# Splitting the row maxima of an attention step as columns on GpSimd before they are turned, and storing them with two transfers

## The reference, cut to what matters

```python
q, k, v = x @ Wq.T, x @ Wk.T, x @ Wv.T           # x: (4, 512, 256) after the layer norm
scores = einsum('bsqhd,bthd->bqhst', qh, kh) * scale     # qh: (4, 512, 4, 8, 8), kh: (4, 512, 8, 8)
probs  = softmax(scores, axis=-1)
a_dot  = einsum('bqhst,bthd->bsqhd', probs, vh)
out    = a_dot * (1 - w) + a_mem * w              # a_mem from elu(q) @ memory
# + moe_forward(x): top 2 of 8 experts (256 -> 1024 -> 512 -> 256) + a shared expert (256 -> 1024 -> 256)
```

## Time and profile before

| | us |
|---|---|
| median of three runs | 819.31 |
| the runs | 809.73 to 820.09 |
| the profiled execution | 819.6 |
| its span, first to last instruction | 817.8 |
| mean granted TensorE clock in it | 0.985 |

### The profile page before, as it was taken

One profiled execution on the slowest core, in us unless ns is written; L12 is line 12 of the kernel. 1 busy time (PEld: TensorE's weight loads), 2 busy tenths in 40 slices (PEclk: granted clock), 3 DMA queues, 4 the chain that ended last, 5 costly groups with the idle time before them and its releaser, 6 DMA issues.

```text
span 817.8 us, 14331 instructions
## 1 busy us (share of the span) xinstructions
PE 711.9 (87%) x3976; PEld 371.2 (45%) x3977; DVE 586.4 (72%) x800; ACT 482.2 (59%) x886; POOL 150.6 (18%) x265
## 2 busy tenths in 40 slices
PE   4999999667788888888888888889999999998997
PEld 2455445211122221122122211368777778777887
DVE  4375688657688888888988884376677676675764
ACT  2473401456678878778877778655556555555422
POOL 1000001746452122211222212000000000003750
PEclk9999999879799999999999999999999999999999
DMA  9637000435320011111011163041111111113431
GB/s 318 212 103 282 30 0 16 139 126 191 100 82 28 19 30 30 30 30 30 16 29 30 43 219 108 13 137 51 50 39 51 51 38 51 46 38 111 123 104 51
DMA packets 51295, 65.36 MB, mean 80 GB/s; under 512 B 9512, under 2 KB 44224, under 8 KB 51264
## 3 DMA queue, kind: packets, MB, share of 16 engines
q1 hardware_dynamic: 40192, 40.85, 15.7%
q10 hardware_dynamic: 8000, 15.73, 5.9%
q0 software_dynamic: 3072, 8.39, 3.3%
HBM read 40.15 MB, written 24.38 MB: 79 GB/s over the span
## 4 chain that ended last, share of the span: by engine, by line
PE 58%; issue 13%; ACT 10%; DVE 7%; POOL 4%; DMA 3%; SPq 3%; DVEq 2%; ACTq 1%; POOLq 0%
PE ps L1374 10%; PE ps L1345 9%; PE ps L1226 7%; ACT att L718 6%; PE ps L1398 6%; PE ps L1476 5%; PE ps L1444 5%; DVE smax L980 4%; PE ps L1218 3%; PE ps L1491 3%; ACT att_r L698 2%; DMA att<-m_parts 2%; SPq L407 2%; PE ps L1251 2%; PE ps L1186 2%
## 5 line engine op out<-in xcount | busy, mean ns | idle before, releaser
L980 DVE TENSOR_REDUCE smax<-ps 128x2 f32<-128x1024 f32 x256 | 302.4, 1221 | 64.5 <-PE ps L1251 62.3
L718 ACT ACTIVATE att<-ps 128x512 f32<-128x512 f32 x512 | 267.7, 602 | 102.0 <-PE ps L1398 100.8
L1398 PE MATMUL ps<-att 51*128 51x512 bf16 x512 | 163.0, 390 | 63.9 <-ACT att L718 23.4
L1251 PE MATMUL ps<-att 48*128 48x512 bf16 x512 | 160.7, 391 | 1.4 <-DVE smax L980 1.4
L1398 PEld LDWEIGHTS ps<-att 51*128 51x128 bf16 x512 | 40.1, 94 | 254.4 <-DVE smax L980 104.0
L1345 PE MATMUL ps<-att,v_head 128*32 128x512 f32 x1024 | 139.2, 616 | 1.6 <-ACT o_sb L677 0.6
L1037 DVE TENSOR_TENSOR att_r<-big,att_r 128x1024 fp32r<-128x1024 f32 x76 | 89.8, 1222 | 60.4 <-ACT att_r L698 60.4
L1374 PE MATMUL ps<-att_r 128*128 128x512 f32 x456 | 115.8, 403 | 15.3 <-DVE att_r L1041 13.6
L1374 PEld LDWEIGHTS ps<-att_r 128*128 128x128 f32 x456 | 84.1, 188 | 39.5 <-issue 19.6
L698 ACT ACTIVATE att_r<-big 128x1024 fp32r x74 | 74.4, 1053 | 19.6 <-issue 17.6
L584 POOL DMA_INDIRECT xn<-slot_y,slot x32 | 33.8, 1056 | 229.1 <-DMA slot_y<-xn 219.6
(11 more groups left out here) (162 smaller groups left out, 711.2 us busy)
## 6 DMA issues: line engine op xcount, KB each, us to landing
big<-w ACTq DMA_DIRECT2D x8, 1024.0 KB, 5.6
q_stacks<-big SPq DMA_DIRECT2D x12, 512.0 KB
att<-q_stacks SPq DMA_DIRECT2D x64, 96.0 KB, 2.1
slot_x<-zeros SPq DMA_DIRECT2D x1, 4992.0 KB, 17.2
e_x<-slot_x SPq DMA_DIRECT2D x39, 128.0 KB, 2.0
slot_y<-xn SPq DMA_DIRECT2D x39, 128.0 KB, 1.7
big<-w ACTq DMA_DIRECT2D x8, 512.0 KB, 8.1
att<-k_stacks SPq DMA_DIRECT2D x64, 48.0 KB, 2.0
```

What stands on the lines that cost most here:

```text
L718: act.activation(probs[:, t % 2, g, :], ps[:, RING[turn_of(u) % 3], :], ACT.Exp, scale=SCALE)\
L980: dve.reduce_max(smax[:, s % 2, :].rearrange("p (half v) -> p half v", half=2)[:, :, v], ps[:, bank:bank + 2, :], X_AXIS).then_inc(max_don ...
L1251: return pe.matmul(ps[:, bank + half, :], q_st[s][rows, g, P * st:P * (st + 1)], k_st[s][rows, :], start=True, stop=True)
L1398: pe.matmul(ps[:, RING[turn % 3], :], k_st[s][rows, P * t:P * (t + 1)], q_st[s][rows, g, :], start=True, stop=True).then_inc(scores_ready, 1)
```

## The change

- transpose_max is now an ordinary bf16 matmul: its stationary operand is max_parts (128 x 48), the moving one `eye`, a bf16 copy of the identity that GpSimd makes at the start. It gives 48 x 128: per half, three parts of eight rows.
- The split stands before it: split_max on GpSimd takes smax as it is (128 partitions x 16) once all eight maxima are there, in the same four operations, each waiting for the one before, and writes the parts into max_parts. It waits for the matmul that read the buffer two steps before.
- negate_max on ScalarE negates 48 x 128 and rounds to bf16 (neg_parts), which is exact. It waits for the transfers that read that buffer.
- m_rows waits for the negation and issues two transfers of three rows instead of six of one.
- On TensorE, in step(), transpose_max comes behind weighted_values of that quarter instead of ahead of it; it waits for the last split operation.
- On GpSimd split_max(i) comes ahead of stage_v(i) and of the scatters instead of between them.
- VectorE's first maximum of a step waits for the split that read the buffer, no longer for the matmul.

```diff
@@ -127,9 +127,11 @@
         expert = sb("expert", [P, TILES], I32)
         mden = sb("mden", [P, 2, 2, G])
         smax = sb("smax", [P, 2, 16])
-        negm = sb("negm", [16, 2, P])
-        negr = sb("negr", [16, 2, P])
-        m_parts = sb("m_parts", [16, 2, 3, P], BF16)
+
+        max_parts = sb("max_parts", [P, 2, 48], BF16)
+        max_rest = sb("max_rest", [P, 16])
+        neg_parts = sb("neg_parts", [48, 2, P], BF16)
+        eye = sb("eye", [P, P], BF16)
         rden = sb("rden", [P, 2, 32])
         oT_sb = sb("oT_sb", [P, 2, 32, DH + 1])
         otmp = sb("otmp", [P, 2, 32, DH])
@@ -207,6 +209,7 @@
         router_zero = sem("router_zero")
         ident_zero = sem("ident_zero")
         ident_ready = sem("ident_ready")
+        eye_ready = sem("eye_ready")
         consts_ready = sem("consts_ready")
         slots_cleared = sem("slots_cleared")
         dve_step = sem("dve_step")
@@ -400,12 +403,11 @@
                       .then_inc(stack_loaded[n], 16)
 
             def m_rows(i, s):
-                sp.wait_ge(m_ready, i + 1)
+                sp.wait_ge(negm_ready, i + 1)
                 for half in range(2):
-                    for c in range(3):
-                        row = HALF * half + R + c
-                        sp.dma_start(q_st[s % 4][row:row + 1, :, :].rearrange("o g s -> o (g s)"),
-                                     m_parts[8 * half:8 * half + 8, s % 2, c, :]).then_inc(m_loaded[s % 2], 16)
+                    first = HALF * half + R
+                    sp.dma_start(q_st[s % 4][first:first + 3, :, :].rearrange("c g n -> c (g n)"),
+                                 neg_parts[24 * half:24 * half + 24, s % 2, :]).then_inc(m_loaded[s % 2], 16)
 
             sp.wait_ge(s_hused, NF)
             load_stack(0, 0, 0)
@@ -480,6 +482,8 @@
             pool.wait_ge(ident_zero, 1)
             pool.affine_select(out=ident[:, :], in_=ident[:, :], compare_op=ALU.not_equal, fill=1.0,
                                base=0, pattern=[[-1, P]], channel_multiplier=1).then_inc(ident_ready, 1)
+            pool.wait_ge(ident_ready, 1)
+            pool.tensor_copy(eye[:, :], ident[:, :]).then_inc(eye_ready, 1)
             pool.memset(router[:, :, :], 0.0).then_inc(router_zero, 1)
             pool.memset(mem_w[:, :], 0.0).then_inc(mem_zero, 1)
             pool.memset(zeros[:, :], 0.0)
@@ -512,19 +516,22 @@
                 pool.tensor_copy(v_head[:, s % 2, :, first:first + DH],
                                  v_all[:, bass.ds(b * ST, ST), bass.ds(h * DH, DH)]).then_inc(v_head_ready, 1)
 
-            def split_m(i, s, pairs):
+            def split_max(i, s):
 
                 a = s % 2
-                pool.wait_ge(negm_ready, i + 1)
-                wait(pool, m_loaded[a], pairs * 96)
-                pool.tensor_tensor(m_parts[:, a, 0, :], negm[:, a, :], zeros[0:16, 0:P], ALU.subtract).then_inc(m_hi, 1)
+                whole, rest = [m.rearrange("p (half v) -> p half v", half=2) for m in (smax[:, a, :], max_rest[:, :])]
+                hi, mid, lo = [max_parts[:, a, :].rearrange("p (half c v) -> p half c v", half=2, c=3)[:, :, c, :]
+                               for c in range(3)]
+                nothing = zeros[:, 0:16].rearrange("p (half v) -> p half v", half=2)
+                pool.wait_ge(max_done, i * 8 + 8)
+                wait(pool, maxT_in_psum, i - 1)
+                pool.tensor_tensor(hi, whole, nothing, ALU.subtract).then_inc(m_hi, 1)
                 pool.wait_ge(m_hi, i + 1)
-                pool.tensor_tensor(negr[:, a, :], negm[:, a, :], m_parts[:, a, 0, :], ALU.subtract).then_inc(m_res, 1)
+                pool.tensor_tensor(rest, whole, hi, ALU.subtract).then_inc(m_res, 1)
                 pool.wait_ge(m_res, i + 1)
-                pool.tensor_tensor(m_parts[:, a, 1, :], negr[:, a, :], zeros[0:16, 0:P], ALU.subtract).then_inc(m_mid, 1)
+                pool.tensor_tensor(mid, rest, nothing, ALU.subtract).then_inc(m_mid, 1)
                 pool.wait_ge(m_mid, i + 1)
-                pool.tensor_tensor(m_parts[:, a, 2, :], negr[:, a, :], m_parts[:, a, 1, :], ALU.subtract)\
-                    .then_inc(m_ready, 1)
+                pool.tensor_tensor(lo, rest, mid, ALU.subtract).then_inc(m_ready, 1)
 
             def add_o(pair, a, b, h):
 
@@ -535,8 +542,8 @@
                                    otmp[:, a, :, :].rearrange("p (t g two) d -> p t g (two d)", t=ST, g=G),
                                    ALU.add).then_inc(o_added, 1)
 
+            split_max(0, 0)
             stage_v(0, 0, 0, 0)
-            split_m(0, 0, 0)
 
 
             pool.wait_ge(s_add, 2 * 4)
@@ -557,8 +564,8 @@
                 for s in range(4):
                     i = blk * 4 + s
                     if not (first and s == 0):
+                        split_max(i, s)
                         stage_v(i, b, h0 + s, s)
-                        split_m(i, s, blk * 2 + s // 2)
                     if isinstance(i, int) and 1 <= i < 8:
                         scatter(*SCATTERS[i])
                     if s == 1 and not first:
@@ -665,10 +672,10 @@
                         between[n, f]()
 
 
-            def negate_max(i, s):
+            def negate_max(i, s, pairs):
                 act.wait_ge(maxT_in_psum, i + 1)
-                wait(act, m_ready, i - 1)
-                act.activation(negm[:, s % 2, :], ps[0:16, RING[MAX_AT % 3], 0:P], ACT.Copy, scale=-1.0)\
+                wait(act, m_loaded[s % 2], pairs * 32)
+                act.activation(neg_parts[:, s % 2, :], ps[0:48, RING[MAX_AT % 3], 0:P], ACT.Copy, scale=-1.0)\
                    .then_inc(negm_ready, 1)
 
             def evacuate_o(pair, a):
@@ -703,7 +710,7 @@
                 for u in range(16):
                     t, g = divmod(u, G)
                     if u == 4 and not last:
-                        negate_max(i + 1, s + 1)
+                        negate_max(i + 1, s + 1, blk * 2 + (s + 1) // 2)
                     if u == 7 and last:
                         act.wait_ge(scattered, 16 * TOPK * NT)
                         copy_ex(0, 0)
@@ -724,7 +731,7 @@
                 act.dma_start(w2_sb[:, n, :, :], w2[n].rearrange("(k p) n -> p k n", p=P)).then_inc(w12_loaded, 16)
 
             LATE = {-4: (4, 5), -3: (6,), -2: (7,), -1: ()}
-            negate_max(0, 0)
+            negate_max(0, 0, 0)
             for i in range(4):
                 exps(0, i, first=i == 0)
                 if i == 0:
@@ -976,7 +983,7 @@
 
                 dve.wait_ge(a_ready, i * 8 + (v + 1))
                 if v == 0:
-                    wait(dve, maxT_in_psum, i - 1)
+                    wait(dve, m_ready, i - 1)
                 dve.reduce_max(smax[:, s % 2, :].rearrange("p (half v) -> p half v", half=2)[:, :, v],
                                ps[:, bank:bank + 2, :], X_AXIS).then_inc(max_done, 1)
 
@@ -1159,6 +1166,7 @@
         @block.tensor
         def _(pe):
             pe.wait_ge(ident_ready, 1)
+            pe.wait_ge(eye_ready, 1)
 
             def transpose_xn(g):
 
@@ -1298,9 +1306,9 @@
                     wait(pe, probs_ready, i * 16 + (v + 1))
 
             def transpose_max(i, s):
-                pe.wait_ge(max_done, i * 8 + 8)
+                pe.wait_ge(m_ready, i + 1)
                 bank_free(i - 1, MAX_AT)
-                pe.transpose(ps[0:16, RING[MAX_AT % 3], 0:P], smax[:, s % 2, :], ident[:, :])\
+                pe.matmul(ps[0:48, RING[MAX_AT % 3], 0:P], max_parts[:, s % 2, :], eye[:, :], start=True, stop=True)\
                   .then_inc(maxT_in_psum, 1)
 
             shared_down(1, NF - 1)
@@ -1378,7 +1386,7 @@
             def step(blk, s, first=False, ahead=True, last=False):
                 i = blk * 4 + s
                 pair = blk * 2 + s // 2
-                pe.wait_ge(m_loaded[s % 2], blk * 192 + 96 * (s // 2 + 1))
+                pe.wait_ge(m_loaded[s % 2], blk * 64 + 32 * (s // 2 + 1))
                 for t in range(ST):
                     for g in range(PAIR):
                         v = PAIR * t + g
@@ -1401,8 +1409,6 @@
                                 ins = max_scores((s + 2) % 4, v, 1 - half, 2 * (v % 2))
                                 if half == 1:
                                     ins.then_inc(a_ready, 1)
-                    if t == MAX_AT // G - 1 and not last:
-                        transpose_max(i + 1, s + 1)
                     if t == OUT_AT // G - 1 and s % 2 == 0 and not first:
                         transpose_o(pair - 1, (s // 2 + 1) % 2)
 
@@ -1410,6 +1416,8 @@
                         weighted_values(i, s, t - 1, pair)
                     elif not first:
                         weighted_values(i - 1, s + 3, ST - 1)
+                    if t == MAX_AT // G - 1 and not last:
+                        transpose_max(i + 1, s + 1)
 
                     if last and t == 0:
                         pe.wait_ge(experts_known, 1)
```

## The result

| | before | after |
|---|---|---|
| median, us | 817.8 (4 runs, 809.73 to 820.09) | 792.14 (4 runs, 791.57 to 793.09) |
| ratio | | 0.9705, 95% interval 0.9635 to 0.9774 |
| the profiled execution, us | 819.6 | 791.59 |
| its span, us | 817.8 | 789.8 |
| mean granted clock | 0.985 | 0.995 |

The kernel is 3.0% faster. 792.14 is 5 us above the forecast of 787 and inside its range. The median of before lies between 809.24 and 817.8 in the sets of runs of this document; those of after, in its two sets, are 0.07 us apart. Of the 28.0 us between the two spans, 17.7 are gained by the start of step 6 (230.69 against 212.97), 9.3 in steps 6 to 27, and 1.0 in the last four steps; behind the attention both kernels take the same time.

What follows compares the result with a forecast made beforehand. No engine is full; steps are chains of hand-overs in a three-bank PSUM ring, with waits for rows. Gains of 20.3 us by step 6, 11.5 in steps 6 to 27 and 0.9 at the end give 787 us; range 778 to 800.

Steps and rivals of the forecast that it cites:

- hidden 0.57 us: Ahead of even loop steps: TensorE waits 0.57 us a pair for row transfers, not the eighth maximum; all of it goes.
- The signs named in the forecast: No row waits ahead of steps 1, 2, 4; full clock 150 to 220 us; 21.2 us pairs; timely split; 2 us gap.
- the risk in its last sentence: Step 0: if the TensorE gap near 148 lowers the clock as long waits did, 1.2 us are lost.
- B: GpSimd's split is late for the turning matmul: 802 us at 0.45 us an operation, 790 at 0.33; chance 0.2.
- D: Same split, each operation far dearer: all gain lost at 0.60 us, 836 us total at 0.74; chance 0.03.
- C: Early steps: rows or stack still land late beside expert load, scatter and stack loads; 797 us, chance 0.12.
- E: Little gain: even steps really wait for the maximum, early waits come from loads beside the rows; 814 us, chance 0.05.
- a quarter of the 0.23 us between two of 512 columns: Turning matmul on TensorE: a bf16 matmul of 128 columns should hold it for 0.06 us.
- The upper bound, 0.21: Turning matmul on TensorE: at most the old turn's 0.21 us, which would cost 31 x 0.15 = 4.7 us.
- the forecast has 139.2: Step 0 on GpSimd: the eight adds start near 139.2 us, when the first memory result is there.
- step 0 lost its 2 us: Step 0: the split for step 1 stands behind the eight adds, so the step grows by 2.1 us.
- 787 if so and 777 if not: Old kernel's 809.73 run: 787 us stays if its 10 us were shorter row waits, 777 if they lie elsewhere.

Runs made afterwards that it cites:

- before_split_first: Old kernel with only GpSimd's order changed, the split ahead of the copy of the values (stage_v): 804.05 us, ratio 0.9891.
- turn_twice: Changed kernel with the turning matmul issued twice in a row: 794.58 us, ratio 0.98.
- after_again: Changed kernel run once more, nothing edited: 792.21 us, ratio 0.9732.
- before_again: Old kernel run once more for a second profile, nothing edited: 814.14 us.
- stage_first: Changed kernel with GpSimd's old order, the copy of the values (stage_v) ahead of split_max: 873.86 us, ratio 1.0746.
- split_early: Changed kernel with GpSimd's split for step 1 put ahead of the eight memory adds: 789.37 us, ratio 0.9779.
- before_loads_late: Old kernel with the expert loads of steps 0 to 3 issued ahead of steps 28 to 31: 820.58 us.
- turn_first: Changed kernel with the turning matmul back ahead of the weighted values, split still on columns: 816.28 us, ratio 1.0105.

## Why the prediction was right, and where its numbers were off

**The mechanism held.** No rows are waited for, steps 1 to 6 run at full clock, the split ends before the matmul's turn, the pair has lost its hidden 0.57 us, and there is a gap of 2.33 us in step 0. The signs named in the forecast are in the profile, but for two: the clock is not full from 150 to 157 us (the risk in its last sentence), and the pair is 21.43 and not 21.2 us. B and D fall with the measured 0.22 us an operation (forecast 0.215) and with the split ready 0.42 us ahead of the turn in odd and 0.72 in even steps (forecast, with the hand-over, 0.32 and 0.59). C falls: the rows of step 1 were down before the load was issued, those of step 2 had 2.0 us to spare beside it (DMA share 0.81 in step 1), and no matmul of scores waited. E falls with `before_split_first`: the wait ahead of even steps was the rows.

**The gap of 4.7 us in the span** (789.8 against 785.1) lies in three places.

- *The turning matmul was sized at 0.06 us and takes 0.17.* The step that failed is "a quarter of the 0.23 us between two of 512 columns". A pair gained 0.85 instead of 1.05: 0.2 x 11 = 2.2 us in steps 6 to 27 and 0.26 us in steps 2 to 5. `turn_twice` shows that the scaling gives about the price of one more such matmul, but a single one pays some 0.1 us besides, between itself and the scores behind it. The Trainium skill, "TensorE: Matmul & The Clock Gate", section "Back-to-back issue gap", has 81 ns in a sustained stream; the 0.08 us between the two here agree, and the lone one is outside what that states. The upper bound, 0.21, was nearer than the value taken, and the argument for the low one rested on a row of scores behind scores.
- *The low clock in step 0*, named as a risk of 1.2 us and left out of the sum: 3.70 us at a granted clock of 0.50 for the quarter at 151.63, against 261.04 - 258.48 = 2.56 at full clock: 1.1 us.
- *The kernel's first part ran 1 us later*: the adds begin at 140.30, the forecast has 139.2. The first four projections took 3.78 us from 12.40 in this profile, and 3.39 in that of before; where the next group of L1171 (before) or L1179 (after) starts, it is 17.25 before, 18.26 after, 18.03 in `after_again`, 16.70 in `before_again` and 18.77 in `before_split_first`, which has nothing changed there; `stage_first` and `turn_twice`, which have the added copy of the identity, are at 16.99 and 17.05. So it comes with the run and not with the change. From there to the start of step 0 all these profiles take the same time within 0.2 us.

2.2 + 0.3 + 1.1 + 1.0 = 4.6 of 4.7 us. The rest of the sum was close: step 1 took 9.74 (9.8), step 0 lost its 2 us, the split's place behind the adds was read rightly and `split_early` gets 2.8 us back.

**The median of before.** The forecast asked whether the 10 us of the run at 809.73 were shorter waits for rows, with 787 if so and 777 if not. That run has no profile. `before_again`, profiled at 812.75, is shorter in that way (6 us less wait, 7.3 us by step 6), which speaks for the first. It follows that the gain depends on which run of before is taken: 28 and 20 us between the two pairs of profiles, 26 and 20 between the medians of the two sets that have both kernels.

**What the forecast didn't price.** It has no term for the order on GpSimd. In the kernel before, the copy of the values held the split back by up to 0.63 us in the odd step (the negation ended at 244.91, the split began at 245.54), and `before_split_first` shows that this alone was worth 0.43 us a pair. `stage_first` shows that the order is a condition of the rest: 82 us without it. And the three parts do not add: the order on GpSimd alone gives 1.1%, the place of the matmul alone nothing, the columns with the matmul in its old place lose 1%; together they give 2.7 to 3.0%. Why `before_split_first` has a first wait of 7.12 us stays open.

**The rule weighed under C.** That rule (the Trainium skill, "DMA: Bandwidth & Descriptors", section "Queues, rings and completion order": an engine takes turns between queue rows a packet at a time) had led me to expect that small transfers would hardly wait; the Trainium skill does not say there how long they wait. `before_loads_late` against before measures 3.2 us ahead of step 1 that the rows wait beside an expert load, and in after the rows of step 2 land 3.3 us after their last issue beside a load, those of step 1 1.2 us without one. Here the measurement decides: the rows are slowed.

## What to carry to other kernels

When work moves into the chain of an engine, look first at what stands ahead of it in the queue of the engine that makes it: the same copy ahead of the same split cost 0.4 us a pair while only transfers hung on it, and about 5 us once a matmul did. A small result that a later step needs is best made early and stored beside work that covers even a disturbed transfer; that removes both the wait and its scatter, and then one transfer more or less is worth nothing. A lone small matmul can cost more than its share of columns (0.17 us here instead of 0.06), so size it from a row that has one in the same place, or keep the upper bound in the sum.

## What the runs showed of the hardware that I had not expected

The granted clock fell from 2.4 to 1.2 GHz, the levels that 1.0 and 0.5 in the rows stand for, with only short idle times before it. In `turn_first` the longest idle times ahead of 276.04 are 0.89 and 0.64 us, with matmuls between them, and the clock of that stretch is 0.68. It is not so each time: of the eleven odd steps from 7 to 27, all with the same work, six have a low stretch. In after, with the 0.89 and no wait for the split, it stays at 1.00 for nine pairs, and so it does before with 0.89 and 0.56. In `split_early` it falls to 0.63 behind several idle times of 0.19 to 0.39 us between 142.7 and 150.9, none long. The clock's price in such a case can be more than half that of the waits: some 11 us beside 13 of added waits for GpSimd in `turn_first`, some 25 beside 48 in `stage_first` (estimates from the lengths of steps with and without a low stretch). A forecast that adds waits alone is then too low; mine for `stage_first` was.
